# Sparse experts in tiles of 256 rows instead of 128, with the splitting of their weights begun during the routing

## The chip, the cores and the metric

One core of a Trainium2 chip runs the whole program in one launch. The metric is the device time of one execution in microseconds (us). The engines are TensorE (PE, with its weight loads as PEld), VectorE (DVE), ScalarE (ACT), GpSimd (POOL) and SyncE (SP, which issues most DMAs here).

## What is computed

The reference is an audio tower: a tokenizer, then four layers of attention (or a state-space scan) and a feed-forward part, over 32 clips of 93 tokens with 256 features. Each part gets the layer norm of the running sum and is added to it. The change concerns the feed-forward part of the third layer, a mixture of 8 experts of which each token uses the best two:

```python
def _L2_ffn_ref(x, Wr, W1, W2):
    xf = x.reshape(-1, d)
    logits = xf @ Wr
    probs = jax.nn.softmax(logits, axis=-1)
    weights, indices = jax.lax.top_k(probs, TOP_K)
    out = jnp.zeros_like(xf)
    for e in range(n_experts):
        h = jax.nn.gelu(xf @ W1[e], approximate=False) @ W2[e]
        coeff = jnp.sum(jnp.where(indices == e, weights, 0.0), axis=-1)
        out = out + coeff[:, None] * h
    return out.reshape(b, t, d)
```

There are 2976 tokens, so 5952 pairs of a token and an expert. W1 is 256 x 1024 and W2 1024 x 256 for each expert, all in f32.

## The kernel before

The layers run one after the other, each in its own block of five instruction streams, with a barrier between blocks. Streams wait for each other on semaphores that are written out by hand. The mixture (`mixture`) is two blocks, `dispatch` and `expert_tiles`, after the differential attention (`differential_attention`).

**Clearing.** `moe_sent` is a buffer in HBM with a place for every row that any expert may get: `TILES` tiles of 128 rows, where `TILES` is the most that 5952 pairs and eight unfilled last tiles can need, 54. Unused places must hold zeros. The differential attention's SP stream clears the whole buffer (L1406) after its own weight loads and ahead of eight small loads of gamma (L1409). All of that layer's engines wait for `w_loaded`, which counts the gamma loads too.

**Routing (`dispatch`).** In eight groups of four clips VectorE normalises rows (L318), TensorE transposes them (L334), ScalarE copies the result out (L342), TensorE multiplies it by the router's weights (L1668) and VectorE copies the logits (L1691, in `route`). Then VectorE does the softmax, picks the best two, and works out each pair's place among the tiles (L1700 to L1742); TensorE ranks the pairs in between (L1678). Tile t belongs to one expert, whose number is put into `expert[t]`.

**Weights (`dispatch`).** Matmuls here are done in bf16 parts: a f32 matrix is the sum of a high and a low bf16 part, and a product is three matmuls (`split_products`, L1546 to L1548: high by high, high by low, low by high). The weights of the experts are loaded in 32 jobs of 512 KB through four staging buffers (SP, L1618 and L1620). For each, ScalarE makes the high part (L1656) and VectorE the low part by a subtraction (L1750, shown as `moe_w<-route_stage,moe_w`); the buffer is then free for the job four later. ScalarE does its 32 after the softmax's exponential. VectorE does one after each clip's rows in the scatter:

```python
for b in range(B):
    if b >= SENDING:
        dve.wait_ge(rows_sent[b % SENDING], 32 * (b // SENDING))
    dve.tensor_scalar(n.xn[rows, b % SENDING, :], hidden[rows, b, :], ...).then_inc(rows_ready, 1)
    dve.wait_ge(high_ready, b + 1)
    dve.tensor_tensor(weights(b, 1), stage[:, b % STAGES, :], weights(b, 0), ALU.subtract).then_inc(low_ready, 1)
```

**Scatter (`dispatch`).** For each clip VectorE normalises the rows again (L1747) into one of four buffers, and GpSimd sends them by two indirect DMAs (L1641), one for each choice, to their places in `moe_sent`.

**Tiles (`expert_tiles`).** SP loads tile t's rows (L1796). TensorE transposes them (`turn`, L1857), ScalarE and VectorE split them into parts (`take`, L1831 and L1903). `into_hidden` makes 8 blocks of 128 hidden features x 128 rows, each over two halves of 256 features, in three matmuls each: 48 matmuls of 128 columns, with W1 as the stationary operand. ScalarE applies the gelu twice to each half of the hidden sums (L1841 in f32, L1842 as the high part), VectorE subtracts for the low part (L1916). `out_of_hidden` multiplies by W2: 8 x 3 = 24 matmuls of 256 columns, with the activations as the stationary operand. VectorE copies the result (`keep`, L1910), SP stores it (L1800) to `moe_back`. TensorE's order in a tile is `into_hidden(t)`, `turn(t + 1)`, `out_of_hidden(t - 1)`; ahead of each of the two products its sequencer loads the expert's number from `expert` into a register (`value_load`), from which the weights' address is computed. The hidden sums have two sets of two banks in PSUM, so a tile's matmuls need not wait for the last tile's gelu. `over_tiles` makes a loop of it, two tiles a pass.

**Gather.** When all tiles are stored, GpSimd fetches each clip's two sets of rows by 64 indirect DMAs (L1821), and VectorE adds them to the running sum with their weights (L1931).

Of the kernel before, what the change touches and what calls it, by code (L numbers as in the profile page):

```python
# [83 lines left out]
def constants(nc, top, shared):  # L84
# [6 lines left out]
    shared["sent"] = nc.dram_tensor("moe_sent", (TILES * P, D), F32, kind="Internal").ap()  # L91
# [1287 lines left out]
def differential_attention(nc, shared, dram):  # L1379
# [5 lines left out]
    with Scope(nc, "dattn") as s:  # L1385
# [167 lines left out]
TILES = (2 * B * T + EXPERTS * (P - 1)) // P  # L1553


def mixture(nc, shared, dram):

    with Scope(nc, "moe") as s:
# [5 lines left out]
        back = nc.dram_tensor("moe_back", (TILES * P, D), F32, kind="Internal").ap()  # L1564
# [4 lines left out]
def dispatch(nc, shared, dram, w1, w2, slot, share, expert):  # L1569
# [4 lines left out]
    with Scope(nc, "route") as s:  # L1574
# [34 lines left out]
        with nc.Block() as block:  # L1609
# [15 lines left out]
            def _(pool):  # L1625
# [12 lines left out]
                for b in range(B):  # L1638
                    pool.wait_ge(rows_ready, b + 1)
                    for k in range(2):  # L1640
                        pool.indirect_dma_start(sent, bass.IndirectOffsetOnAxis(slot[0:T, k, b:b + 1], 0),  # L1641
                                                n.xn[0:T, b % SENDING, :], None, bounds_check=TILES * P - 1
# [40 lines left out]
            def _(dve):  # L1683
# [3 lines left out]
                def route(g, last):  # L1687
                    if not last:
                        norm_group_dve(dve, n, g + 1, hidden)
# [3 lines left out]

                over_groups(dve, route)
# [14 lines left out]
                dve.sem_inc(chosen_ready, 1)  # L1709

# [8 lines left out]
                steps.link(dve.tensor_scalar(x, upto[:, :, B - 1], 1.0 / P, 1.0 - 1.0 / P - 0.5 + 0.5 / P, ALU.mult, ALU.add))  # L1719
# [4 lines left out]
                steps.link(dve.tensor_scalar(first_slot, x, float(P), None, ALU.mult))  # L1724
# [19 lines left out]
                for b in range(B):  # L1744
# [4 lines left out]
                    dve.wait_ge(high_ready, b + 1)  # L1749
                    dve.tensor_tensor(weights(b, 1), stage[:, b % STAGES, :], weights(b, 0), ALU.subtract).then_inc(low_ready, 1)  # L1750
# [3 lines left out]
def expert_tiles(nc, shared, w1, w2, slot, share, expert, back):  # L1754

    hidden, ident, sent = (shared[k] for k in ("hidden", "ident", "sent"))
    BANK = FC // 2
    RING = 8
    with Scope(nc, "tiles") as s:
        x_in = s.sb("x_in", [P, 2, D])  # L1760
        x_part = s.sb("x_part", [P, 2, 2, DC, P], BF16)
        gelu = s.sb("gelu", [P, 2, BANK, P])
        act1 = s.sb("act1", [P, 2, 2, FC, P], BF16)
        y = s.sb("y", [P, 2, D])
# [25 lines left out]
        with nc.Block() as block:  # L1790
            @block.sync
            def _(sync):
# [12 lines left out]
                def tile(t, j, last):  # L1805
                    if not isinstance(t, int) or t < TILES - 2:
                        load(t + 2, j)
                    if later(t, 1):
                        store(t - 1, 1 - j)
# [848 lines left out]
```

## Time and profile before

| | us |
|---|---|
| median of 3 runs (lowest to highest) | 4664.99 (4653.47 to 4668.2) |
| the profiled execution | 4662.15 |
| its span, first to last instruction | 4660.4 |
| TensorE matmuls busy | 3329.6 (71%) |
| TensorE weight loads busy | 2177.4 (47%) |
| VectorE busy | 2352.3 (50%) |
| GpSimd busy | 1287.5 (28%) |
| ScalarE busy | 1128.7 (24%) |
| routing (2090 to 2155), scatter (2155 to 2285) | 65, 130 |
| expert tiles (2285 to 2749), gather (2749 to 2865) | 464, 116 |

The profile is of one execution. Busy shares are averages over stages that have different limits; a stage's own limit is read from its stretch. Matmuls overlap each other in the array, so the distance between the starts of two of them says more than the duration in their row, whose end is modelled. The idle time in brackets behind a row is that of its engine just before it, with what ended it. "issue" is time in which an engine waited for nothing that the profile shows.

### The profile page before, as it was taken

To read this page: it belongs to the slowest core of one execution; us is meant where nothing else is said; L and a number is where in the kernel's file an instruction comes from. 1 tells how busy PE (TensorE), PEld (TensorE's weight loads), DVE (VectorE), ACT (ScalarE), POOL (GpSimd) and SP (SyncE) were. 2 spreads that over 40 slices of the span, in tenths; PEclk is the share of its full clock that TensorE was granted. 3 is DMA by queue.
4 is the path that set the end of the run, shared out by engine and by line. 5 is a ranking of instruction groups with operands and counts; after the bars stand their busy time and mean duration, and the time that the engine had idled before them with its cause. 6 is when DMAs were issued, how large, how long until landed. Compare 5 with 4: busy or idle time off the path is not lost. (4 is left out here: it accounts for less than half of the span.)

```text
span 4660.4 us, 73226 instructions
## 1 busy us (share of the span) xinstructions
PE 3329.6 (71%) x24055; PEld 2177.4 (47%) x24056; DVE 2352.3 (50%) x4014; ACT 1128.7 (24%) x2258; POOL 1287.5 (28%) x902
## 2 busy tenths in 40 slices
PE   7599935589948999982388852455645565559999
PEld 3367722267735777762266631122222232235677
DVE  0444464234342555544322223788998899861343
ACT  2221200112112222212222210333433343313222
POOL 0111201012110333334400035444554455520121
PEclk9798857778879999995699985677877787769999
DMA  1000003700020000003311111111211121110000
GB/s 41 11 1 0 0 2 70 98 8 0 0 80 0 0 0 0 0 12 100 98 32 32 32 37 50 40 46 34 53 33 40 33 53 33 47 34 0 5 11 11
DMA packets 248269, 136.98 MB, mean 29 GB/s; under 512 B 176065, under 2 KB 224259, under 8 KB 248176
## 3 DMA queue, kind: packets, MB, share of 16 engines
q1 hardware_dynamic: 228272, 119.66, 10.6%
q0 software_dynamic: 18432, 12.40, 1.1%
q10 hardware_dynamic: 1472, 3.85, 0.3%
q8 instruction: 37, 0.61, 0.1%
q14 instruction: 56, 0.46, 0.0%
HBM read 102.36 MB, written 33.31 MB: 29 GB/s over the span
## 5 line engine op out<-in xcount | busy, mean ns | idle before, releaser
L2214 PE MATMUL ssm_y<-ssm_hC,top_ident 128*128 128x512 f32 (+1 forms) x768 | 461.2, 749 | 433.4 <-DVE ssm_hC L2298 432.8
L2083 POOL TENSOR_TENSOR ssm_dBx<-ssm_du,ssm_bc 128x1488 f32<-128x1488 f32 x128 | 543.1, 4255 | 323.2 <-DVE ssm_state L2292 254.8
L2214 PEld LDWEIGHTS ssm_y<-ssm_hC,top_ident 128*128 128x128 f32 x768 | 174.7, 242 | 685.0 <-DVE ssm_hC L2298 457.9
L2292 DVE TENSOR_TENSOR_SCAN ssm_state<-ssm_dA,ssm_dBx 128x744 f32<-128x744 f32 x256 | 421.9, 1689 | 24.7 <-POOL ssm_dBx L2083 11.4
L2155 ACT ACTIVATE ssm_dA<-ssm_delta,ssm_decay 128x368 f32<-128x368 f32 x512 | 270.2, 561 | 657.3 <-DVE ssm_state L2292 565.2
L2298 DVE TENSOR_TENSOR ssm_hC<-ssm_state,ssm_bc 128x1488 f32<-128x1488 f32 x128 | 224.6, 1755 | 4.4
L1821 POOL DMA_INDIRECT tiles_got<-moe_back,moe_slot x64 | 91.5, 1430 | 488.8 <-issue 484.2
L1546 PE MATMUL tiles_hidden<-tiles_x_part,moe_w 128*128 128x128 bf16 x864 | 197.5, 229 | 25.2 <-issue 22.8
L657 ACT ACTIVATE dattn_probs<-dattn_scoresT 93x372 f32<-93x372 f32 x256 | 108.1, 472 | 418.4 <-PE dattn_scoresT L570 418.4
L677 DVE TENSOR_REDUCE dattn_negmax<-dattn_scores 93x4 f32<-93x372 f32 x256 | 127.1, 536 | 161.8 <-PE dattn_scores L542 161.8
L1548 PE MATMUL tiles_hidden<-tiles_x_part,moe_w 128*128 128x128 bf16 x864 | 197.4, 229 | 0.0
L1547 PE MATMUL tiles_hidden<-tiles_x_part,moe_w 128*128 128x128 bf16 x864 | 190.3, 220 | 0.0
L584 PE MATMUL dattn_outputs<-dattn_v,dattn_probs 93*93 (+1 forms) x2048 | 185.8, 233 | 0.0
L584 PEld LDWEIGHTS dattn_outputs<-dattn_v,dattn_probs 93*93 93x93 f32 x2048 | 181.9, 163 | 3.4
L1916 DVE TENSOR_TENSOR tiles_act<-tiles_gelu,tiles_act 128x512 bf16<-128x512 f32 x108 | 74.8, 693 | 212.4 <-ACT tiles_act L1842 212.4
L501 POOL TENSOR_TENSOR rattn_q<-rattn_q_all,rattn_only 128x372 f32<-128x372 f32 x64 | 51.8, 809 | 442.9 <-PE rattn_scoresT L570 246.7
L1420 POOL TENSOR_TENSOR dattn_square<-dattn_square,top_minus_half 93x16 f32<-93x16 f32 x32 | 92.7, 2897 | 290.8 <-DVEq L1496 290.8
L2226 PE MATMUL ssm_misc<-ssm_w_out,ssm_xc 128*93 128x256 f32 x256 | 95.8, 555 | 100.4 <-DVEq L2320 73.8
L501 POOL TENSOR_TENSOR eattn_q<-eattn_q_all,eattn_only 128x372 f32<-128x372 f32 x64 | 51.7, 808 | 404.0 <-PE eattn_scoresT L570 217.0
L501 POOL TENSOR_TENSOR dattn_q<-dattn_q_all,dattn_only 128x744 f32<-128x744 f32 x64 | 91.7, 1433 | 208.6 <-PE dattn_scoresT L570 117.0
L501 POOL TENSOR_TENSOR gattn_q<-gattn_q_all,gattn_only 128x372 f32<-128x372 f32 x64 | 51.8, 809 | 332.4 <-PE gattn_scoresT L570 247.9
L1546 PE MATMUL tiles_product<-moe_w,tiles_act 128*128 x432 | 118.2, 274 | 27.6 <-issue 27.5
(533 smaller groups left out, 7333.6 us busy)
## 6 DMA issues: line engine op xcount, KB each, us to landing
ssm_bc<-dbc_rows SPq DMA_DIRECT2D x128, 372.0 KB, 4.1
route_stage<-in_L_ffn_W SPq DMA_DIRECT2D x32, 512.0 KB, 4.4
qkv_rows<-rattn_rows SPq DMA_DIRECT2D x32, 288.0 KB, 3.0
rattn_heads<-qkv_rows SPq DMA_DIRECT2D x96, 96.0 KB, 3.5
moe_sent<-top_blank SPq DMA_DIRECT2D x1, 6912.0 KB, 20.8
tiles_x_in<-moe_sent SPq DMA_DIRECT2D x54, 128.0 KB, 2.0
moe_back<-tiles_y SPq DMA_DIRECT2D x54, 128.0 KB, 1.7
tok_frames<-in_frames ACTq DMA_DIRECT2D x8, 376.0 KB, 8.5
```

The costliest lines, as they stand in the source:

```text
L501: pool.tensor_tensor(a.q[:, buf, c, :, :], a.q_all[:, c, bass.ds(b * T, T)].unsqueeze(1).broadcast_to([P, a.variants, T]), a.only[:, :].un ...
L584: mm = pe.matmul(a.ps_o[0:T, bank, h * (HD + 1):(h + 1) * (HD + 1)], a.probs[0:T, w % 4, j * T:(j + 1) * T], a.v[0:T, b, h, :], start=True ...
L657: act.activation(a.probs[0:T, w % 4, :], a.ps_t[0:T, w % 2, 0:GT], ACT.Exp, scale=a.exp_scale).then_inc(a.probs_ready, 1)
L677: dve.tensor_reduce(a.negmax[0:T, a.first_map(w):a.first_map(w) + 4], a.ps_s[0:T, w % 2, 0:GT].rearrange("p (j t) -> p j t", j=4), AX.X, A ...
L1546: pe.matmul(out, w_high, x_high, start=start, stop=False)
L1547: pe.matmul(out, w_high, x_low, start=False, stop=False)
L1548: return pe.matmul(out, w_low, x_high, start=False, stop=stop)
L2083: pool.tensor_tensor(dBx[:, k % 2, :, :], du[:, :, :], bc[:, q % 2, 0, k % 2, :].unsqueeze(1).broadcast_to([P, CC, GT]), ALU.mult).then_in ...
L2155: ins = act.activation(dA[:, half, c * GT:(c + 1) * GT].rearrange("p (u t) -> p u t", u=GU)[:, :, 1:], delta[:, 2 * half + c, :].rearrange ...
L2214: mm = pe.matmul(ps_y[:, at], ident[:, :], hC[:, k % 2, :, :].rearrange("p c t -> p (c t)")[:, at], start=(k == 0), stop=(k == N - 1))
L2292: dve.tensor_tensor_scan(state[:, k % 2, chunks, :].rearrange("p c t -> p (c t)"), dA[:, half, 0:HALF], dBx[:, k % 2, chunks, :].rearrange ...
L2298: dve.tensor_tensor(hC[:, k % 2, :, :], state[:, k % 2, :, :], bc[:, q % 2, 1, k % 2, :].unsqueeze(1).broadcast_to([P, CC, GT]), ALU.mult) ...
```

## The change

A tile has 256 rows (`ROWS`), held as two halves of 128 (`HALVES`), and there are 31 tiles, whatever the routing. `moe_sent` and `moe_back` have 7936 rows instead of 6912. In `expert_tiles` a hidden block is 128 features x 256 rows; the hidden sums of one tile fill four banks, of which there is one set; gelu and subtraction work on a bank of two blocks at a time (the same 128x512 shape); the product is made for each half of the rows. TensorE and the other engines still loop over two tiles; SP's stream is written out.

In `dispatch` eight of the 32 splits are moved into the routing loop, one after each group, on ScalarE (`high`) and VectorE (`low`); these loops are written out. VectorE does two more ahead of its wait for the ranks. The other 22 follow the rows of the first 22 clips in the scatter.

```diff
-TILES = (2 * B * T + EXPERTS * (P - 1)) // P
+HALVES = 2
+ROWS = HALVES * P
+TILES = (2 * B * T + EXPERTS * (ROWS - 1)) // ROWS
...
                 sync.dma_start(shared["sent"].rearrange("(a p) d -> p a d", p=P),
-                               shared["blank"][:, :].unsqueeze(1).broadcast_to([P, TILES, D])).then_inc(sent_clear, 16)
+                               shared["blank"][:, :].unsqueeze(1).broadcast_to([P, TILES * HALVES, D])).then_inc(sent_clear, 16)
...
             def _(act):
-                with act.Fori(0, G) as g:
+                def high(k):
+                    act.wait_ge(stage_loaded[k % STAGES], 16 * (k // STAGES + 1))
+                    act.activation(weights(k, 0), stage[:, k % STAGES, :], ACT.Copy).then_inc(high_ready, 1)
+
+                for g in range(G):
                     act.wait_ge(routed, GU * g)
                     norm_group_act(act, n, g, ps_x)
+                    high(g)
                 act.wait_ge(prob_in, 1)
                 act.activation(prob[0:T, :, :], logits[0:T, :, :], ACT.Exp).then_inc(prob_exp, 1)
-                for k in range(JOBS):
-                    act.wait_ge(stage_loaded[k % STAGES], 16 * (k // STAGES + 1))
-                    act.activation(weights(k, 0), stage[:, k % STAGES, :], ACT.Copy).then_inc(high_ready, 1)
+                for k in range(G, JOBS):
+                    high(k)
...
+                def low(k):
+                    dve.wait_ge(high_ready, k + 1)
+                    dve.tensor_tensor(weights(k, 1), stage[:, k % STAGES, :], weights(k, 0), ALU.subtract).then_inc(low_ready, 1)
+
+                for g in range(G):
+                    if g < G - 1:
                         norm_group_dve(dve, n, g + 1, hidden)
                     dve.wait_ge(routed, GU * g + GU)
                     dve.tensor_copy(logits[0:T, bass.ds(GU * g, GU), :],
                                     ps_l[0:T, 0:GU * E].rearrange("p (u e) -> p u e", e=E)).then_inc(logits_ready, 1)
-
-                over_groups(dve, route)
+                    low(g)
...
                 dve.sem_inc(chosen_ready, 1)
+                for k in (G, G + 1):
+                    low(k)
...
-                    dve.wait_ge(high_ready, b + 1)
-                    dve.tensor_tensor(weights(b, 1), stage[:, b % STAGES, :], weights(b, 0), ALU.subtract).then_inc(low_ready, 1)
+                    if G + 2 + b < JOBS:
+                        low(G + 2 + b)
...
-    BANK = FC // 2
+    BANKS, PER = 4, FC // 4
-        ps_h = s.ps("hidden", [P, 2, 2, BANK, P])
-        ps_y = s.ps("product", [P, 2, 512])
+        ps_h = s.ps("hidden", [P, BANKS, PER, ROWS])
+        ps_y = s.ps("product", [P, 2, HALVES, D])
...
                 def into_hidden(t, j):
                     e = pe.value_load(expert[0:1, bass.ds(t, 1)], min_val=0, max_val=EXPERTS - 1)
                     pe.wait_ge(x_low, t + 1)
-                    for half in range(2):
-                        if later(t, 2):
-                            pe.wait_ge(act_high, 2 * t + (half - 3))
-                        for f in range(half * BANK, (half + 1) * BANK):
+                    for q in range(BANKS):
+                        if later(t, 1):
+                            pe.wait_ge(act_high, BANKS * t + (q + 1 - BANKS))
+                        for f in range(PER * q, PER * (q + 1)):
...
-                    for f in range(FC):
-                        if f % BANK == 0:
-                            pe.wait_ge(act_low, 2 * t + (f // BANK + 1))
+                    for h in range(HALVES):
+                        for f in range(FC):
+                            if h == 0 and f % PER == 0:
+                                pe.wait_ge(act_low, BANKS * t + (f // PER + 1))
+                            mm = split_products(pe, ps_y[:, j, h, :], [act1[:, j, part, f, h * P:(h + 1) * P] for part in range(2)],
+                                                [w2[:, part, bass.ds(e, 1), f, :].rearrange("p a n -> p (a n)") for part in range(2)],
+                                                f == 0, f == FC - 1)
```

Three places in the order of the instructions. First SP's queue in the differential attention, where the buffer is cleared:

```order
 L755 DMA dattn_lam<-in_L_attn_lambda_q 93x8
 L755 DMA dattn_lam<-in_L_attn_lambda_k 93x8
-L1406 DMA moe_sent<-top_blank 128x54x256
+L1406 DMA moe_sent<-top_blank 128x62x256
 L1409 DMA dattn_gamma<-in_L_attn_gamma 16x1 x8
 L1399 UNCONDITIONAL_BRANCH
```

Nothing moved; the clearing DMA writes 62 blocks of 128 rows instead of 54, and the gamma loads stand behind it as before.

Second VectorE at the end of the routing's groups, before (the first rows are the end of the loop, `route_logits` are the router's scores, L1700 begins the softmax):

```order
L1691 ISA
L1691 COPY route_logits<-route_scores 93x32
L324 REGISTER_ALU
L324 COMPARE_AND_BRANCH
L1691 COPY route_logits<-route_scores 93x32
L1700 TENSOR_REDUCE route_total<-route_logits 93x32
L1701 TENSOR_TENSOR route_logits<-route_logits,route_total 93x256
L1704 TENSOR_REDUCE route_total<-route_prob 93x32
```

and now:

```order
L318 TENSOR_SCALAR route_xn<-top_hidden,route_mean,route_rstd 93x256 x4
L1701 COPY route_logits<-route_scores 93x32
L1695 TENSOR_TENSOR moe_w<-route_stage,moe_w 128x1024
L1701 COPY route_logits<-route_scores 93x32
L1695 TENSOR_TENSOR moe_w<-route_stage,moe_w 128x1024
L1709 TENSOR_REDUCE route_total<-route_logits 93x32
L1710 TENSOR_TENSOR route_logits<-route_logits,route_total 93x256
L1713 TENSOR_REDUCE route_total<-route_prob 93x32
```

A split (L1695) stands behind each copy of logits, the last one ahead of the softmax's first step.

Third TensorE in a pass of the tile loop, from the last hidden matmuls of a tile to the first product matmuls, before:

```order
L1548 MATMUL tiles_hidden<-tiles_x_part,moe_w 128x128
L1853 ISA
L1857 MATMUL tiles_xturned<-top_ident,tiles_x_in 128x128 x2
L1875 ISA
L1875 TENSOR_LOAD moe_expert
L1875 ISA x2
L1880 ISA
L1546 ISA
L1546 MATMUL tiles_product<-moe_w,tiles_act 128x256
```

and now:

```order
L1548 MATMUL tiles_hidden<-tiles_x_part,moe_w 128x256
L1860 ISA
L1865 MATMUL tiles_xturned<-top_ident,tiles_x_in 128x128 x4
L1883 ISA
L1883 TENSOR_LOAD moe_expert
L1883 ISA x2
L1889 REGISTER_ALU
L1546 ISA
L1546 MATMUL tiles_product<-moe_w,tiles_act 128x256
```

The order is the same; the hidden matmuls have 256 columns, there are four transposes, and the register load (TENSOR_LOAD) stands ahead of the product as before. A pass of the loop has 266 rows of this list before and 320 now.

## Rows read from the trace of the kernel before

**Rows 1.** Stretches (scatter, steady tiles): us, busy us of PE, PEld, DVE, ACT, POOL (x instructions), granted clock, DMA

```profile
2155.00:2285.00 130.00, 0.00 (x0) 0.00 (x0) 51.12 (x63) 29.58 (x28) 105.16 (x64) 0.50 0.57 161
...
2420.00:2520.00 100.00, 88.72 (x880) 68.67 (x879) 26.39 (x47) 28.15 (x58) 0.00 (x0) 1.00 0.10 31
```

**Rows 2.** Timeline, TensorE, first and last tile: start us, us, engine, line, operation [idle before]

```profile
2289.07 0.29 PE L1546 MATMUL tiles_hidden<-tiles_x_part,moe_w 128*128 128x128 bf16 x1 [1.02 <-DVE tiles_x_part L1903]
...
2293.20 0.26 PE L1546 MATMUL tiles_hidden<-tiles_x_part,moe_w 128*128 128x128 bf16 x1
...
2745.89 0.27 PE L1548 MATMUL tiles_product<-moe_w,tiles_act 128*128 x1
```

**Rows 3.** Timeline, TensorE, one tile of the loop

```profile
2320.85 0.23 PE L1546 MATMUL tiles_hidden<-tiles_x_part,moe_w 128*128 128x128 bf16 x1 [0.75 <-issue]
...
2325.17 0.41 PE L1857 MATMUL tiles_xturned<-top_ident,tiles_x_in 128*128 128x128 f32 x2
2326.14 0.28 PE L1546 MATMUL tiles_product<-moe_w,tiles_act 128*128 x1 [0.56 <-issue]
...
2329.22 0.23 PE L1546 MATMUL tiles_hidden<-tiles_x_part,moe_w 128*128 128x128 bf16 x1 [0.25 <-issue]
```

**Rows 4.** Timeline, TensorE, within a hidden and a product phase

```profile
2500.92 0.23 PE L1546 MATMUL tiles_hidden<-tiles_x_part,moe_w 128*128 128x128 bf16 x1
...
2501.92 0.23 PE L1546 MATMUL tiles_hidden<-tiles_x_part,moe_w 128*128 128x128 bf16 x1
...
2504.31 0.27 PE L1546 MATMUL tiles_product<-moe_w,tiles_act 128*128 x1
...
2506.49 0.27 PE L1548 MATMUL tiles_product<-moe_w,tiles_act 128*128 x1
```

**Rows 5.** Timeline, TensorE, end of the stage: hidden to product, product to product

```profile
2739.52 0.23 PE L1548 MATMUL tiles_hidden<-tiles_x_part,moe_w 128*128 128x128 bf16 x1
2740.43 0.28 PE L1546 MATMUL tiles_product<-moe_w,tiles_act 128*128 x1 [0.68 <-issue]
...
2742.96 0.27 PE L1548 MATMUL tiles_product<-moe_w,tiles_act 128*128 x1
2743.35 0.28 PE L1546 MATMUL tiles_product<-moe_w,tiles_act 128*128 x1
```

**Rows 6.** Scatter: GpSimd in the timeline; groups by line (busy us, mean ns | idle before)

```profile
2155.48 5.82 POOL L1641 DMA_INDIRECT moe_sent<-route_xn,moe_slot  x1 [57.09 <-issue]
...
2174.53 2.12 POOL L1641 DMA_INDIRECT moe_sent<-route_xn,moe_slot  x1 [0.30 <-DVE route_xn L1747]
...
L1641 POOL DMA_INDIRECT moe_sent<-route_xn,moe_slot x64 | 105.2, 1643 | 76.3 <-issue 72.0 <-DVE route_xn L1747 4.3
L1750 DVE TENSOR_TENSOR moe_w<-route_stage,moe_w 128x1024 bf16<-128x1024 f32 x32 | 38.7, 1211 | 0.0
```

**Rows 7.** Groups by line in the tile stage, ScalarE

```profile
L1842 ACT ACTIVATE tiles_act<-tiles_hidden 128x512 bf16<-128x512 f32 x108 | 64.5, 597 | 0.0
...
L1831 ACT ACTIVATE tiles_x_part<-tiles_xturned 128x256 bf16<-128x256 f32 x54 | 20.7, 384 | 98.0 <-PE tiles_xturned L1857 98.0
```

**Rows 8.** DMA issues of the page (KB each, us to landing); timeline, VectorE, attention layer

```profile
moe_sent<-top_blank SPq DMA_DIRECT2D x1, 6912.0 KB, 20.8
...
1391.09 0.16 DVE L1460 TENSOR_TENSOR dattn_lam<-dattn_lam 93x8 f32<-93x8 f32 x1 [24.46 <-DMA dattn_gamma<-in_L_attn_gamma]
```

**Rows 9.** DMA issues of the page: loads of a tile

```profile
tiles_x_in<-moe_sent SPq DMA_DIRECT2D x54, 128.0 KB, 2.0
```

**Rows 10.** Timeline, routing: ScalarE, VectorE in a group; VectorE after the ranks

```profile
2125.49 0.85 ACT L342 ACTIVATE route_xT<-route_xturned 128x372 f32<-128x372 f32 x2 [4.10 <-PE route_xturned L334]
2125.64 1.38 DVE L318 TENSOR_SCALAR route_xn<-top_hidden,route_mean,route_rstd 93x256 f32 x4 [1.18 <-PE route_xturned L334]
...
2144.18 0.42 DVE L1715 COPY route_choice_left<-route_rank 93x256 f32<-93x256 f32 x1 [2.23 <-PE route_rank L1678]
```

**Rows 11.** DMA queues, tile stage: packets, MB, share of 16 engines

```profile
q8 instruction: 5, 0.08, 0.1%
```

More of the change, by code:

```diff
@@ L1795, in load @@
                         sync.wait_ge(x_turned, t - 1)
-                    sync.dma_start(x_in[:, j, :], sent[bass.ds(t * P, P), :]).then_inc(x_loaded[j], 16)
+                    sync.dma_start(x_in[:, j, :, :], rows_of(sent, t)).then_inc(x_loaded[j], 16)
                 def store(t, j):
                     sync.wait_ge(y_copied, t + 2)
-                    sync.dma_start(back[bass.ds(t * P, P), :], y[:, j, :]).then_inc(y_stored[j], 16)
+                    sync.dma_start(rows_of(back, t), y[:, j, :, :]).then_inc(y_stored[j], 16)
                 load(0, 0)
                 load(1, 1)
[L1805 to L1809, printed above, removed]
-                over_tiles(sync, tile)
-                store(TILES - 1, 1)
+                for t in range(TILES):
+                    if t < TILES - 2:
+                        load(t + 2, t % 2)
+                    if t:
+                        store(t - 1, (t - 1) % 2)
+                store(TILES - 1, (TILES - 1) % 2)
             @block.gpsimd
@@ L1829, in take @@
                     if later(t, 2):
[L1830 to L1832 removed]
+                        act.wait_ge(h_done, BANKS * (t - 1))
+                    act.activation(x_part[:, j, 0, :, :], ps_x[:, j, :, :], ACT.Copy).then_inc(x_high, 1)
                 def tile(t, j, last):
[L1835 to L1838 removed]
+                    for q in range(BANKS):
+                        act.wait_ge(h_done, BANKS * t + (q + 1))
+                        if later(t, 1) or q >= 2:
+                            act.wait_ge(act_low, BANKS * t + (q - 1))
                         if later(t, 2):
                             act.wait_ge(y_done, t - 1)
[L1841 to L1844 removed]
+                        act.activation(gelu[:, q % 2, :, :], ps_h[:, q, :, :], ACT.Gelu)
+                        act.activation(act1[:, j, 0, PER * q:PER * (q + 1), :], ps_h[:, q, :, :], ACT.Gelu).then_inc(act_high, 1)
+                        if q == BANKS - 2 and not last:
                             take(t + 1, 1 - j)
@@ L1877, in out_of_hidden @@
                         pe.wait_ge(y_copied, t)
[L1878 to L1883 removed]
+                    for h in range(HALVES):
+                        for f in range(FC):
[4 more added lines that the diff above has]
+                                                f == 0, f == FC - 1)
                     mm.then_inc(y_done, 1)
@@ L1909, in keep @@
                         dve.wait_ge(y_stored[j], 8 * (t - j))
-                    dve.tensor_copy(y[:, j, :], ps_y[:, j, 0:D]).then_inc(y_copied, 1)
+                    dve.tensor_copy(y[:, j, :, :], ps_y[:, j, :, :]).then_inc(y_copied, 1)
                 def tile(t, j, last):
-                    for half in range(2):
-                        dve.wait_ge(act_high, 2 * t + (half + 1))
-                        at = slice(half * BANK, (half + 1) * BANK)
-                        dve.tensor_tensor(act1[:, j, 1, at, :], gelu[:, half, :, :], act1[:, j, 0, at, :],
+                    for q in range(BANKS):
+                        dve.wait_ge(act_high, BANKS * t + (q + 1))
+                        at = slice(PER * q, PER * (q + 1))
+                        dve.tensor_tensor(act1[:, j, 1, at, :], gelu[:, q % 2, :, :], act1[:, j, 0, at, :],
                                           ALU.subtract).then_inc(act_low, 1)
-                        if half == 0 and not last:
+                        if q == BANKS - 2 and not last:
                             take(t + 1, 1 - j)
```

60 lines of the change are left out of this document (22 added, 38 removed).

## The prediction

> **What bounds the kernel now.** I read the profile's first line, then the table of stretches, then the rows of each stretch that the change touches. The span is 4660.4 us and the execution's own time 4662.15 us, 2.8 us under the median of the runs shown (4664.99 us); the sum below is made against 4662.15. Between runs 0.3% (14 us) is about what this kernel's measurement can tell from no change.
>
> Three stretches are touched. In the tile stage the reader is to see TensorE busy 88.72 us of 100 at a granted clock of 1.00, the others under a third [rows 1]: TensorE sets the pace. It runs from the first hidden matmul at 2289.07 to the start of the last product matmul at 2745.89 [rows 2], so 54 tiles take 456.9 us with the last matmul's pitch, 8.46 us each. In the scatter before it, TensorE has nothing to do and GpSimd is busy 105.16 us of 130 [rows 1] with 64 indirect DMAs [rows 6]: GpSimd sets the pace there. And the attention layer before (differential_attention) starts only when VectorE has the gamma loads, for which it waits 24.46 us [rows 8].
>
> **Inside a tile.** A tile has 48 hidden matmuls of 128 columns, 2 transposes, 24 product matmuls of 256 columns. Hidden start to transposes is 4.32 us, transposes to product 0.97, product to the next hidden 3.08 [rows 3]. From 2500.92 to 2501.92 twelve hidden matmuls start: 0.083 us each. From 2504.31 to 2506.49 twenty product matmuls: 0.109 us each [rows 4]. Why are 128 columns not half of 256? At the end of the stage hidden matmuls are followed directly by a product: last start 2739.52, next 2740.43, 0.91 us, which is 0.83 more than a pitch. Two products follow each other with 0.39 us (2742.96 to 2743.35), 0.28 more than a pitch [rows 5]. Both times the same register load of the expert's number stands between. I read this so: TensorE's instruction stream needs 0.083 us per matmul. Hidden matmuls of 128 columns wait for it, so no lead builds up and the load is paid in full (0.83). Product matmuls of 256 columns take 0.109 in the array, the stream gains 24 x 0.026 = 0.62 us on it, and pays only the rest (0.83 - 0.62 = 0.21, measured 0.28).
>
> **The change, tile stage.** 54 tiles of 74 TensorE operations (3996) become 31 of 100 (3100). Every matmul now has 256 columns.
> - Hidden: 48 x 0.109 = 5.23 us.
> - Transposes: 4 instead of 2. The two take 0.41 us as one row [rows 3] with the modelled tail in it; I take 0.7 for four (bounds 0.5 and 0.85).
> - Product: 2 halves x 24 x 0.109 = 5.23 us.
> - Gaps: before, 0.97 - 0.41 = 0.56 ahead of the product and 3.08 - 24 x 0.109 = 0.46 ahead of the hidden matmuls [rows 3]. Now the stream gains 48 x 0.026 = 1.25 us in each phase, more than the 0.83 that a load costs, so both gaps should be covered: 0.2 us are left for both. Upper bound: both stay, 1.0.
>
> Sum 5.23 + 0.7 + 5.23 + 0.2 = 11.4 us a tile (bounds 11.0 and 12.3); x 31 = 353 us. The nearest row for the gap is the product followed by a product, where a lead of 0.62 took away two thirds; a lead of 1.25 is twice that.
>
> What must stay hidden: the hidden sums now have one set of four banks, so TensorE must not overtake ScalarE. ScalarE's two passes over 512 columns take 0.597 us each [rows 7], four banks 4.8 us, and the copy of x (0.384 for 256 columns, about 0.6 for 512) makes 5.4 of 11.4. The last bank is read only after the next tile's transposes, by about 8 us into the tile, and TensorE wants that bank 11.4 + 3.9 us into it: 7 us of slack. The loads of x (2.0 us for 128 KB [rows 9], at most twice that for 256 KB) stand in SP's queue behind the store of an older tile and still have more than a tile's time. If this cover were gone, each us would be paid 31 times.
>
> Edges, once: the stage starts cold. From 2289.07 to 2293.20, 39 matmuls start [rows 2], 0.106 each, after a stretch at clock 0.50, the 1.2 GHz level [rows 1]. With 256 columns that time passes at an estimated 0.213, some 2 us lost; the second tile's wait for its x (1.02 us before, in the same row's place) grows to about 1.6; the first load and copies are 1.3 longer, the last copy and store 0.7. Together 6 us. Stage: 353 + 6 = 359 against 457: **-98 us.**
>
> Here a rule speaks for another pace. The measured row is 0.109 us for 256 columns [rows 4]. The Trainium skill, TensorE: Matmul & The Clock Gate, section Back-to-back issue gap, gives about 81 ns at 128 columns and 131 at 512 in a real stream of loads and matmuls. The trace agrees at 128 (0.083), but a straight line between the two would be 98 ns at 256, an estimate of that page, and the trace has 109. By the page the tile would be 1.1 us shorter and the whole 33 us; the measured row decides.
>
> **The change, scatter.** Each of 64 issues costs 1.31 + 0.30 us where nothing disturbs it, 103 us; busy and idle of the group without the first wait make 105.2 + 76.3 - 57.1 = 124.4 [rows 6]. The first issue accounts for 4.5 of the excess (5.82, while VectorE runs its first burst of four rows and four weight parts), which stays. The other 16.5 us lie in issues of 2.1 to 2.6 us like the one at 2174.53, which starts right after VectorE's row copy, as VectorE goes on with a weight part (0.81 longer). Of 28 weight parts in the steady loop 18 remain: 16.5 x 10/28 = 5.9, taken as **-5 us**. Bounds: nothing, if the loads of the weights and not VectorE lengthen the issues, and -13 (ten times 1.3).
>
> **The change, routing.** Eight splits go into the routing loop. ScalarE idles 4.10 us a group there and VectorE 1.18 after its logits copy [rows 10]; VectorE's half of a split takes 1.21 us [rows 6], and ScalarE's, one pass over the same 128x1024, is far under 4. So they are hidden but for some 0.05 us of VectorE's, which delay rows that TensorE wants later still; their cover is TensorE's chain of scores and transposes. Only the eighth stands between the last copy and the softmax: +1.2 us. Two more fill VectorE's wait of 2.23 us for the ranks [rows 10] and need 2.4: +0.2. The table of tiles is shorter (31 columns for 54): -0.4. **+1 us.** The weight loads that SP sends earlier land while the queue is otherwise empty.
>
> **The change, clearing.** moe_sent grows from 6912 to 7936 KB. The eight gamma loads stand behind it in SP's queue; it lands after 20.8 us and VectorE starts right behind [rows 8]. 20.8 x 8/54 = **+3 us**, all on the path (bounds 0 and 3.5). The gather after the stage has the same 64 indirect DMAs: nothing.
>
> Sum: -98 - 5 + 1 + 3 = -99. 4662 - 99 = 4563 us; with the 2 to 3 us to the median, **4564 us.**
>
> **The rivals.**
> 1. *The gaps stay* (a register load costs its time whatever the lead). A tile is 12.3 us, 31 x 0.9 = 28 us more: 4592. For it: a product followed by a product still shows 0.28 us [rows 5]. Against: that 0.28 is a third of the 0.83 without lead. If the pauses of the hidden phase stay as well (4.32 - 48 x 0.083 = 0.34 for two halves, 0.7 for four banks), 22 us more: 4614.
> 2. *A hidden matmul of 256 columns is faster than a product one*, because its pace is set by the stream and not by the array. Between the 0.083 and the 0.109 [rows 4] lies 0.096; in the hidden phase alone that is 31 x 48 x 0.013 = 19 us less, 4545, and in both phases 39 us, 4525. Against it stands the steady 0.109 of twenty matmuls with the same number of columns. The page's figure above points this way.
> 3. *The loop no longer stays in the instruction buffer.* TensorE's loop over two tiles grows from 266 to 320 rows of the list of instructions. Before, 25 passes brought only 5 instruction fetches of 16 KB in the whole stage [rows 11], so the loop was not fetched again. If it were now, each of 14 passes would pay up to three fetches in series, 2.0 us each by the nearest row, a small load [rows 9]: 84 us, 4648. The Trainium skill, Runtime: NRT & Kernel Launch, Instruction fetch mechanics, says that a taken branch to code outside the buffer forces a fetch, and gives TensorE a larger buffer (128 KiB) than the other engines in one line and two 16 KiB lines in another; the few fetches here agree with a loop that fits.
> 4. *The splits begun early give nothing*: the scatter is bound by its own issue or its DMAs. 4569; inside the forecast's range.
> 5. *Slower: the clock.* If TensorE were granted 1.2 GHz in the tile stage, a matmul would take an estimated 0.213 and a tile 11.4 + 96 x 0.104 = 21.4 us: 310 us more, 4874. It decides from 99/310, about a third, of the stage at the low level. Its place would be a wait for x or for ScalarE in every tile, long enough to idle TensorE. For it: the stage starts at that level after an idle stretch. Against: the clock stayed at 1.00 with two gaps of half a us in every tile [rows 1], and now there are fewer gaps.
>
> **How the numbers follow.** Forecast 0.66 (own range 4545 to 4576, from the bounds of transposes and scatter); gaps stay 0.15, pauses too 0.05; faster matmuls 0.05; refetching 0.04; nothing from the early splits 0.03; clock 0.02. The range 4544 to 4600 holds the forecast, the gaps that stay and rival 4: 0.84. Over 0.3% faster is all but the clock and part of the refetching: 0.95; within 0.3% 0.02; slower 0.03.
>
> **What would show it.** Right: hidden matmuls at 0.109, a tile period of 11.2 to 11.7 us at clock 1.00, no issue gaps of half a us ahead of product or hidden; undisturbed issues of 1.31 us in the last ten pairs of the scatter; gamma about 3 us later. Wrong: periods of 12.3 us or more, VectorE or ScalarE named as releaser of hidden matmuls, or instruction fetches in every pass.

## The result and the profile after

| us | before | changed |
|---|---|---|
| median (lowest to highest) | 4665.84 (4653.47 to 4668.2, 4 runs) | 4544.84 (4541.94 to 4550.9, 4 runs) |
| span of the profiled execution | 4660.4 | 4541.6 |
| ratio of the times, 95% interval | | 0.9748, 0.9727 to 0.9768 |

The change saves 121 us; 99 to 101 were forecast. The time lies 19 us under the forecast, inside the range of 4544 to 4600 by 0.8 us; two of the four runs (4541.94 and 4543.29) lie below it.

The table of stretches of the changed kernel, scatter and steady tiles, to be read against [rows 1] (us, busy us of PE, PEld, DVE, ACT, POOL with their instructions, granted clock, DMA share, GB/s):

```profile
2148.00:2275.00 127.00, 0.00 (x0) 0.00 (x0) 39.89 (x55) 19.01 (x18) 101.16 (x64) 0.50 0.44 123
...
2400.00:2500.00 100.00, 100.00 (x919) 90.04 (x917) 37.55 (x55) 44.37 (x83) 0.00 (x0) 1.00 0.16 49
```

TensorE was busy 88.72 us of 100 and is now busy all of them, at a clock of 1.00. Its timeline shows the start of the stage, then one steady tile, then the stage's last row (start, us, engine, line, operation, idle before); [rows 2, 3] answer to them:

```profile
2280.77 0.39 PE L1546 MATMUL tiles_hidden<-tiles_x_part,moe_w 128*128 128x256 bf16 x1 [1.50 <-DVE tiles_x_part L1912]
...
2284.58 0.36 PE L1546 MATMUL tiles_hidden<-tiles_x_part,moe_w 128*128 128x256 bf16 x1
2284.77 0.27 PE L1547 MATMUL tiles_hidden<-tiles_x_part,moe_w 128*128 128x256 bf16 x1
...
2290.03 0.28 PE L1546 MATMUL tiles_hidden<-tiles_x_part,moe_w 128*128 128x256 bf16 x1 [1.50 <-DVE tiles_x_part L1912]
...
2453.79 0.27 PE L1546 MATMUL tiles_hidden<-tiles_x_part,moe_w 128*128 128x256 bf16 x1
...
2459.03 0.60 PE L1865 MATMUL tiles_xturned<-top_ident,tiles_x_in 128*128 128x128 f32 x4
2459.47 0.27 PE L1546 MATMUL tiles_product<-moe_w,tiles_act 128*128 x1
...
2464.71 0.27 PE L1546 MATMUL tiles_hidden<-tiles_x_part,moe_w 128*128 128x256 bf16 x1
...
2622.24 0.27 PE L1548 MATMUL tiles_product<-moe_w,tiles_act 128*128 x1
```

The steady tile takes 2464.71 - 2453.79 = 10.92 us: 5.24 + 0.44 + 5.24. That is 100 operations of 0.109 us with nothing between them; the pauses of half a us in [rows 3] are gone. The last product starts at 2622.24, so 31 tiles take 341.6 us where 54 took 456.9: -115.3. The cold start is the 0.21 us pitch of the first 18 matmuls, at a granted clock of 0.50 (the 1.2 GHz level).

The scatter's group by line (busy us, mean ns | idle before), to [rows 6]:

```profile
L1643 POOL DMA_INDIRECT moe_sent<-route_xn,moe_slot x64 | 101.2, 1581 | 77.4 <-issue 74.1 <-DVE route_xn L1758 3.4
```

The clearing among the DMA issues (KB, us to landing), to [rows 8]:

```profile
moe_sent<-top_blank SPq DMA_DIRECT2D x1, 7936.0 KB, 23.6
```

VectorE's timeline at the start of the attention layer, in a routing group and at the ranks, to [rows 8, 10]:

```profile
1385.37 0.16 DVE L1460 TENSOR_TENSOR dattn_lam<-dattn_lam 93x8 f32<-93x8 f32 x1 [27.17 <-DMA dattn_gamma<-in_L_attn_gamma]
...
2102.45 0.19 DVE L1701 COPY route_logits<-route_scores 93x32 f32<-93x32 f32 x1 [2.22 <-PE route_scores L1674]
2102.56 1.21 DVE L1695 TENSOR_TENSOR moe_w<-route_stage,moe_w 128x1024 bf16<-128x1024 f32 x1
...
2136.58 2.36 DVE L1695 TENSOR_TENSOR moe_w<-route_stage,moe_w 128x1024 bf16<-128x1024 f32 x2 [0.15 <-DVE route_chosen L1530]
2138.86 0.42 DVE L1726 COPY route_choice_left<-route_rank 93x256 f32<-93x256 f32 x1
```

GpSimd's issues take 101.2 us where they took 105.2. VectorE waits 27.17 us for gamma, 2.71 more. In the routing it still waits 2.22 us for TensorE after a split, so that split was hidden; the copy of the ranks is no longer waited for.

Stage by stage in the two profiles (first to last row of each): routing 64.2 to 65.3, scatter 124.4 to 120.4, from there to the first hidden matmul 9.2 to 10.8, tiles -115.3, gather 118.2 to 116.5. With the 2.7 of the clearing that is -115.6 us of the 118.8 by which the two spans differ. The other 3 us lie in layers that the change doesn't touch, within the scatter of the profiles: over the 14 profiles of this study the attention layer begins at 1354.5 to 1370.3 us, and the state-space layer takes 1270 to 1280.

### The profile page after: what moved, and what is told of

The parts are those of the page before. It is cut to its first block and busy times, and to the rows that moved or that the text cites. A ratio compares the mean times of both kernels' runs of the same rounds, so it can differ in the third digit from the quotient of the medians.

```text
span 4541.6 us, 69496 instructions
## 1 busy us (share of the span) xinstructions
PE 3260.2 (72%) x23159; PEld 2164.5 (48%) x23160; DVE 2360.9 (52%) x3984; ACT 1144.9 (25%) x2267; POOL 1283.4 (28%) x902
## 5 line engine op out<-in xcount | busy, mean ns | idle before, releaser
L2300 DVE TENSOR_TENSOR_SCAN ssm_state<-ssm_dA,ssm_dBx 128x744 f32<-128x744 f32 x256 | 421.8, 1688 | 24.4 <-POOL ssm_dBx L2091 11.4
L501 POOL TENSOR_TENSOR dattn_q<-dattn_q_all,dattn_only 128x744 f32<-128x744 f32 x64 | 91.6, 1431 | 210.2 <-PE dattn_scoresT L570 115.6
L1924 DVE TENSOR_TENSOR tiles_act<-tiles_gelu,tiles_act 128x512 bf16<-128x512 f32 x124 | 85.8, 692 | 101.8 <-ACT tiles_act L1850 101.8
L1546 PE MATMUL tiles_hidden<-tiles_x_part,moe_w 128*128 128x256 bf16 x496 | 136.2, 274 | 3.0 <-DVE tiles_x_part L1912 3.0
L1547 PE MATMUL tiles_hidden<-tiles_x_part,moe_w 128*128 128x256 bf16 x496 | 136.1, 274 | 0.0
L1548 PE MATMUL tiles_hidden<-tiles_x_part,moe_w 128*128 128x256 bf16 x496 | 136.1, 274 | 0.0
L1547 PE MATMUL tiles_product<-moe_w,tiles_act 128*128 x496 | 135.2, 273 | 0.0
```

What stands on the lines that cost most here:

```text
L501: pool.tensor_tensor(a.q[:, buf, c, :, :], a.q_all[:, c, bass.ds(b * T, T)].unsqueeze(1).broadcast_to([P, a.variants, T]), a.only[:, :].un ...
L1546: pe.matmul(out, w_high, x_high, start=start, stop=False)
L1547: pe.matmul(out, w_high, x_low, start=False, stop=False)
L1548: return pe.matmul(out, w_low, x_high, start=False, stop=stop)
L2300: dve.tensor_tensor_scan(state[:, k % 2, chunks, :].rearrange("p c t -> p (c t)"), dA[:, half, 0:HALF], dBx[:, k % 2, chunks, :].rearrange ...
```

## Experiments on the tile stage

The table is worked out from the traces. Tile stage is from the first hidden to the last product matmul; the phases are medians from start to start.

| run | median us | ratio to before (95%) | tile stage | hidden | transposes | product |
|---|---|---|---|---|---|---|
| before | | | 456.8 | 4.29 | 0.89 | 3.11 |
| keep_before | 4619.31 | 0.9904 (0.9882 to 0.9925) | 410.7 | 4.30 | 0.33 | 2.85 |
| fixed_before | 4517.31 | 0.969 (0.9666 to 0.9714) | 300.4 | 2.68 | 0.22 | 2.62 |
| changed | 4544.84 | 0.9748 (0.9727 to 0.9768) | 341.5 | 5.24 | 0.44 | 5.24 |
| keep_after | 4540.41 | 0.9744 (0.9714 to 0.9773) | 340.9 | 5.24 | 0.44 | 5.24 |
| loads2 | 4549.97 | 0.9764 (0.9735 to 0.9793) | 348.7 | 5.24 | 0.51 | 5.28 |
| loads3 | 4586.6 | 0.9843 (0.9814 to 0.9871) | 386.2 | 5.25 | 1.32 | 5.74 |
| narrow | 4542.79 | 0.9745 (0.9714 to 0.9776) | 345.3 | 5.36 | 0.44 | 5.24 |
| narrow_twin | 4643.56 | 0.9963 (0.9939 to 0.9987) | 434.3 | 7.92 | 0.88 | 5.26 |

**Is it the instruction stream?** On the kernel before, both phases took the first expert's weights, so the choice of the expert is left out, and with it every register load and address step of the tiles:

```diff
-e = pe.value_load(expert[0:1, bass.ds(t, 1)], min_val=0, max_val=EXPERTS - 1)
+e = 0
```

> The kernel before with the first expert's weights for every tile: neither register loads nor address arithmetic in TensorE's stream; which expert computes a row is left out. My theory (the 0.083 us of a hidden matmul is the pace of the instruction stream, two address steps for three matmuls): hidden matmuls at about 0.055 us, no gaps of half a us, a tile of 5.4 to 6 us instead of 8.46, 130 to 165 us less, about 4515 us. Rival (0.083 is what the array needs for a weight load and 128 columns): only the loads go, some 45 us less, hidden matmuls stay at 0.083.

The timeline of one of its tiles, with the last hidden matmul as second row:

```profile
2452.11 0.22 PE L1546 MATMUL tiles_hidden<-tiles_x_part,moe_w 128*128 128x128 bf16 x1
...
2454.73 0.22 PE L1548 MATMUL tiles_hidden<-tiles_x_part,moe_w 128*128 128x128 bf16 x1
2454.79 0.39 PE L1857 MATMUL tiles_xturned<-top_ident,tiles_x_in 128*128 128x128 f32 x2
2455.02 0.27 PE L1546 MATMUL tiles_product<-moe_w,tiles_act 128*128 128x256 bf16 x1
```

The same 48 hidden matmuls take 2.62 us for 47 pitches, 0.056 each. So 0.083 was not the array's pace with 128 columns; the rival falls. The tile stage is 156 us shorter than before: 87 of these lie in the hidden phases, 36 between the transposes and the product, 33 from the product to the next hidden matmul. It is even 41 us shorter than the changed kernel's: 54 x 128 = 6912 rows are less work than 31 x 256 = 7936. The change thus trades 156 us of loads and address steps for 41 us of work on 1024 more rows that stay unfilled; that is its 115.

**Is a load paid before, and covered now?** The register that the hidden phase loaded is kept for the product, in both kernels:

```diff
-e = pe.value_load(expert[0:1, bass.ds(t, 1)], min_val=0, max_val=EXPERTS - 1)
+e = pe.snap(kept[j], min_val=0, max_val=EXPERTS - 1)
```

> The kernel before with one register load less in a tile: the expert's number that was loaded ahead of the hidden matmuls is kept in one of two registers for the product of the same tile, and the range checks of the loads are gone. My theory (hidden matmuls of 128 columns wait for the instruction stream, so a load behind them is paid in full): the time from the transposes to the product falls from 0.97 to about 0.35 us, 0.6 us in 54 tiles, 33 us less, and up to 45 with the checks. Rival (the gap is a wait for the split activations or for the turned x): no change.

> The changed kernel with one register load less in a tile, the same edit as on the kernel before. My theory (the loads are covered): no change, tile period 10.92 us. Rival (a part of a load is still paid): 31 x 0.1 us or more less.

One edit, two answers: 46 us of tile stage in the kernel before (0.57 us at the transposes and 0.27 in the product phase, 54 times), 0.6 us in the changed one. Both as expected. The edit also takes out the range checks, so the 46 us are the price of one load and of the checks of two.

**How much does the lead cover?** The loads were done twice and three times (a loop around the same line).

> The changed kernel with every register load of the expert's number done twice. My theory (the stream gains 0.026 us on the array in each matmul of 256 columns and so covers what stands in it): an extra load is 0.65 to 0.83 us of stream, a tile's stream 10.9 to 11.6 us against 10.92 in the array: nothing to 22 us more. Rival (a load shows in full whatever the lead): 2 x 0.65 to 0.83 in 31 tiles, 40 to 51 us more.

> The changed kernel with every register load done three times. My theory: a tile's stream is now 12.2 to 13.3 us and sets the pace instead of the array: 40 to 73 us more, and the gaps ahead of hidden and product matmuls are back, while matmuls between them stay at 0.109 us or are still at the array's pace after a gap. Rival 1 (a load shows in full): 81 to 103 us more. Rival 2 (loads are always hidden beside matmuls of 256 columns): no change.

A tile of loads3, from its timeline:

```profile
2464.54 0.60 PE L1865 MATMUL tiles_xturned<-top_ident,tiles_x_in 128*128 128x128 f32 x4
2465.93 0.28 PE L1546 MATMUL tiles_product<-moe_w,tiles_act 128*128 x1 [0.78 <-DVE tiles_act L1926]
...
2471.09 0.27 PE L1548 MATMUL tiles_product<-moe_w,tiles_act 128*128 x1
2471.60 0.28 PE L1546 MATMUL tiles_hidden<-tiles_x_part,moe_w 128*128 128x256 bf16 x1 [0.24 <-issue]
```

The pauses are back. The profile names a VectorE step for the first of them, but only the loads differ from the changed kernel, so they are its cause. The step from two to three loads costs (386.2 - 348.7) / 31 / 2 = 0.60 us each; the step from one to two costs 0.12 each. So a phase covers one load and nearly a second, no more. Both rivals (always paid, always hidden) fall.

Why no more, the loads themselves show. The trace has them as instructions of TensorE's sequencer (PEldq), which runs the stream ahead of the array. The loads ahead of one product in the kernel before, in the changed kernel and in loads3 (count, duration in ns, first and last start):

```profile
L1875 PEldq TENSOR_LOAD <-moe_expert x1: 297/297/297, 2325.3 to 2325.3; - x1
```

```profile
L1883 PEldq TENSOR_LOAD <-moe_expert x1: 302/302/302, 2457.8 to 2457.8; - x1
```

```profile
L1885 PEldq TENSOR_LOAD <-moe_expert x3: 296/297/299, 2463.8 to 2465.1; - x3
```

In the kernel before the load starts behind the last hidden matmul and 0.84 us ahead of the first product matmul at 2326.14 [rows 3]: there is no lead, and the load is paid. In the changed kernel it starts 1.7 us ahead of the product at 2459.47, with 15 matmuls and transposes still to start. Over all its tiles from the third on the lead at a load is 13 to 17 of them. In narrow (below), with hidden matmuls half as wide, it is 15 to 17 ahead of the product as well, though that is only 0.98 to 1.20 us. So the lead ends at some 17 matmuls, at either width. Loads done again follow each other at about 0.65 us. In loads3 the first product matmul starts 2.15 us after the first load, and a lead of 11 or 12 matmuls of 0.109 covers 1.2 to 1.3 us of it. What is left is the pause (1.32 us from the transposes to the product, where the changed kernel has 0.44).

**Width or count?** Each hidden matmul of the changed kernel was cut into two of 128 columns:

```diff
-for c in range(DC):
-    mm = split_products(..., x_part[:, j, part, c, :], ...)
+for h, c in ((h, c) for h in range(HALVES) for c in range(DC)):
+    mm = split_products(..., x_part[:, j, part, c, h * P:(h + 1) * P], ...)
```

> The changed kernel, tiles of 256 rows, with each hidden matmul cut into two of 128 columns: 96 instead of 48 in a tile, everything else the same. My theory (the width of the matmuls is what matters): 96 x 0.083 = 8.0 us for the hidden phase, the load ahead of the product shows again with about 0.6 us, a tile of about 14.1 us, 31 x 3.2 = 99 us more than the changed kernel, some 4645 us. Rival (the gain comes from having fewer tiles, with fewer loads, waits and transposes): at most 20 us more.

A miss: 96 matmuls of 128 columns take 5.36 us, 0.056 each, and the time doesn't change. My theory of a price per matmul falls. The rival's number came true, but fewer loads, waits and transposes can't be the whole reason, since in fixed_before the hidden phase itself fell from 4.29 to 2.68 us. The order of TensorE's instructions in narrow tells what I had missed; each ISA row works out an address from the expert's number:

```
L1546 ISA
L1546 MATMUL tiles_hidden<-tiles_x_part,moe_w 128x128
L1547 MATMUL tiles_hidden<-tiles_x_part,moe_w 128x128
L1548 ISA
L1548 MATMUL tiles_hidden<-tiles_x_part,moe_w 128x128
L1546 MATMUL tiles_hidden<-tiles_x_part,moe_w 128x128
L1547 MATMUL tiles_hidden<-tiles_x_part,moe_w 128x128
L1548 MATMUL tiles_hidden<-tiles_x_part,moe_w 128x128
```

The second half of the rows uses the addresses of the first: 32 steps for 96 matmuls, where the kernel before has 32 for 48. The new theory is a price per address step: 3 matmuls of 0.083 have two steps, 0.124 each. narrow_twin keeps everything of narrow and only makes the second half work its addresses out again:

```diff
+pe.reg_mov(copy, e)
+twin = (e, pe.snap(copy, min_val=0, max_val=EXPERTS - 1))
...
-w1[:, part, bass.ds(e, 1), c, f * P:(f + 1) * P]
+w1[:, part, bass.ds(twin[h], 1), c, f * P:(f + 1) * P]
```

> As narrow, 96 hidden matmuls of 128 columns in a tile of 256 rows, but the second half of the rows takes the weights' addresses from a copy of the register, so that they are worked out again: 64 address steps in a hidden phase instead of 32; matmuls, waits and data are the same. My theory after narrow (not a matmul costs stream time but an address step, 0.124 us each): the hidden phase grows from 5.36 to 64 x 0.124 = 7.9 us and a little more, the load ahead of the product finds no lead and shows with 0.6 to 0.7 us, a tile takes about 14.4 us instead of 11.04, 31 x 3.4 = 105 us more than narrow, some 4645 us, tile stage about 448 us. Rival (128 columns are cheap whenever a tile has 256 rows, through the banks or the shape of the phase): no change against narrow, 4543 us.

One tile of narrow, then one of narrow_twin:

```profile
2463.12 0.22 PE L1546 MATMUL tiles_hidden<-tiles_x_part,moe_w 128*128 128x128 bf16 x1
...
2468.48 0.61 PE L1865 MATMUL tiles_xturned<-top_ident,tiles_x_in 128*128 128x128 f32 x4
2468.92 0.27 PE L1546 MATMUL tiles_product<-moe_w,tiles_act 128*128 x1
```

```profile
2499.68 0.22 PE L1546 MATMUL tiles_hidden<-tiles_x_part,moe_w 128*128 128x128 bf16 x1
...
2507.22 0.63 PE L1865 MATMUL tiles_xturned<-top_ident,tiles_x_in 128*128 128x128 f32 x4
2508.09 0.28 PE L1546 MATMUL tiles_product<-moe_w,tiles_act 128*128 x1 [0.24 <-issue]
...
2513.35 0.22 PE L1546 MATMUL tiles_hidden<-tiles_x_part,moe_w 128*128 128x128 bf16 x1
```

The hidden phase is 7.54 us here and 7.93 in the next tile, in turn, against 64 x 0.124 = 7.94. The pause ahead of the product is back (0.87 from the transposes, 0.44 in narrow). Same matmuls, same tiles, same waits, and 89 us more in the tile stage, 434 us where 448 were expected; that the whole, 4643.56 us, comes so close to the expected 4645 is luck. So address steps set the pace of the hidden phase, and tiles of 256 rows use each step for twice the rows. With keep_before it follows that the kernel before was bound by its address steps (the 87 us of the hidden phases) and by the register loads between the phases (most of the other 69).

## Experiments on the scatter and the clearing

tiles_only takes the early splits out of the changed kernel (all 32 follow the rows again); splits_only puts them into the kernel before; after_again is the changed kernel, measured beside the others.

> The changed kernel without the early splits: all 32 splits follow the rows of the scatter again, as before. If the tiles carry the gain (my theory), the tile stage stays at a period of 10.92 us and about 341 us, the scatter is back at 124 us (120 with the early splits), the routing back at 64 us (65), so 3 us more than the changed kernel, some 4548 us. If the early splits carried a part that the stages hide (rival), the time is more than 10 us above the changed kernel's.

> The kernel before with the early splits alone, tiles of 128 rows. My theory: routing 1 us longer, scatter 4 us shorter, tile stage 457 us as before: 3 us less, 4662 us, not to be told from no change by its time. Rival: the early splits carry a share of the change's 121 us: more than 10 us less.

> The changed kernel once more, as the yardstick for the three others: 4545 us within 10, tile period 10.92 us, scatter 120.4 us, routing 65.3 us.

| run | median us (lowest to highest) | ratio to before (95%) | routing | scatter |
|---|---|---|---|---|
| tiles_only | 4559.01 (4548.48 to 4562.62) | 0.9767 (0.9748 to 0.9786) | 64.1 | 128.7 |
| splits_only | 4661.53 (4651.49 to 4671.46) | 0.9996 (0.9984 to 1.0008) | 65.8 | 119.0 |
| after_again | 4546.12 (4544.4 to 4549.45) | 0.9741 (0.9724 to 0.9757) | 65.3 | 120.4 |
| gamma_first | 4536.22 (4526.77 to 4543.22) | 0.9721 (0.9701 to 0.9741) | 65.3 | 120.2 |
| two_splits | 4534.96 (4531.22 to 4543.29) | 0.9717 (0.97 to 0.9735) | 66.4 | 115.2 |

after_again repeats the changed kernel's time and stages. The tiles carry the gain: alone they leave 97.7% of the time, and the splits alone can't be told from no change. By its median tiles_only is 13 us slower than after_again, more than the rival's 10, and the stages explain 7 of it (1.2 less in the routing, 8.3 more in the scatter). The intervals of the two overlap, and the two profiled executions lie the other way round (4548.48 and 4549.45), so it stays open whether the early splits carry more than that beside tiles of 256 rows. In the kernel before they don't (splits_only). Over all profiles the scatter takes 124.4 to 128.7 us with 32 splits beside it (four runs) and 118.2 to 122.3 with 22 (nine runs): the early splits are worth some 6 us there, and cost 1 in the routing. That the splits beside them lengthen GpSimd's issues is plain in the last 20 issues of the changed kernel, which have none left: 1.31 to 1.43 us each and 32.2 in all, where the kernel before took 36.4 and tiles_only 38.6.

gamma_first puts the eight gamma loads ahead of the clearing in SP's queue (two statements change places), and two_splits does two splits in each routing group besides (`high(2 * g)`, `high(2 * g + 1)`, and `low` likewise).

> The changed kernel with the eight gamma loads ahead of the clearing in SP's queue. If the clearing lies on the path (my theory), VectorE's wait for gamma of 27.17 us shrinks by the most of the clearing's 23.6 us, down to what the weight loads and GpSimd's constants (until about 16 us into the layer) leave: 10 to 18 us less in the attention layer, some 4530 us. Rival: the layer's weight loads end just as late, and nothing is gained.

> As the kernel with gamma first, and two splits in each routing group instead of one, so that 18 instead of 10 are done before the scatter. If VectorE's weight parts lengthen GpSimd's issues (my theory), 14 instead of 22 of them are left beside the scatter, which then takes about 117 us instead of 120.4; VectorE's wait of 2.2 us in each routing group covers the second split's 1.21 us, so the routing is at most 2 us longer. Rival: the weights' loads cannot follow (1 MB in a group of 5 us), and the routing grows by more than the scatter shrinks.

VectorE and GpSimd at the start of the attention layer in gamma_first:

```profile
1363.85 0.16 DVE L1460 TENSOR_TENSOR dattn_lam<-dattn_lam 93x8 f32<-93x8 f32 x1 [7.73 <-DMA dattn_gamma<-in_L_attn_gamma]
...
1365.12 7.37 DVE L318 TENSOR_SCALAR dattn_xn<-top_hidden,dattn_mean,dattn_rstd 93x256 f32<-93x256 f32 x4
...
1365.75 6.10 POOL L452 TENSOR_SCALAR_AFFINE_SELECT dattn_sel<-dattn_sel 128x2976 bf16<-128x2976 bf16 x2
```

The wait for gamma falls by 19.4 us, so the clearing was on the path. But the four row copies behind it, 1.38 us in the changed kernel, now meet GpSimd's mask and take 7.37. The layer takes 718.6 us here and 714.2 in two_splits, against 723.0 to 731.1 in the twelve profiles with the old order, 725 in the middle: a gain of 6 and 11 us, where 10 to 18 were expected. What VectorE no longer waits for gamma it loses in part to the mask. In two_splits the scatter takes 115.2 us (about 117 were expected) and the routing is 1 longer, as expected. Its slowest run is 1.1 us faster than the fastest of after_again, and its median 11 us: the best kernel of the study with the full computation, though the 95% intervals of the two ratios overlap. Its gain over gamma_first is not shown by the times.

## Why the prediction was right, and where it was off

- **What bounds** held: TensorE sets the pace of the tile stage (before, its instruction stream; now, the array); GpSimd that of the scatter, VectorE's wait for gamma the start of the attention layer. The sign named for the scatter came true (the last 20 issues above). That for the tile, a period of 11.2 to 11.7 us, did not.
- **Hidden and product phases**, 5.23 us each: measured 5.24.
- **Mis-sized: "Transposes ... I take 0.7 for four (bounds 0.5 and 0.85)" and "0.2 us are left for both" gaps.** Four transposes take 0.44, 0.109 each as every other operation: the 0.41 of the row for two held the modelled tail, and I had not taken it off. Both gaps are nothing. The tile is 10.92 us and not 11.4, below my lower bound of 11.0; 31 x 0.48 = 15 us of the 19. So the time lies inside the range by luck: it is below the forecast's own range of 4545 to 4576, and the bounds from which that was taken (0.5 and 0.85 for the transposes, nothing and -13 for the scatter) give only 4550 to 4574.
- **Mis-sized: the edges**, "together 6 us". 341.6 - 31 x 10.92 = 3 us inside the stage, with the cold pitch and the second tile's wait for x (1.50 in the row at 2290.03, 1.6 expected); the 1.6 us more ahead of it are given back by a gather 1.7 shorter.
- **Failed in its reason: "TensorE's instruction stream needs 0.083 us per matmul".** The runs show 0.124 for an address step, of which three matmuls need two. The sum didn't suffer, and that was luck: the changed kernel happens to have 32 steps in a hidden phase, and 32 x 0.124 make the same 4.0 us as 48 x 0.083, beside matmuls of twice the columns. What I worked out from it for narrow did. "The stream gains 48 x 0.026 = 1.25 us" was right in kind, as both gaps are covered, but not in its reason: the lead is 13 to 17 matmuls (1.44 to 1.95 us) in both phases, and ends there although the 16 steps of a product phase (2.0 us of 5.24) would let it grow further.
- **128 and 256 columns.** The kernel before had 0.083 us at 128 columns; without address steps (fixed_before), or with 32 for 96 matmuls (narrow), they take 0.056, and at 256 columns at 0.109. The Trainium skill, TensorE: Matmul & The Clock Gate, section Back-to-back issue gap, gives about 81 ns at 128 columns for a stream of loads and matmuls. The row's 0.083 agreed with it by accident, and the 0.056 does not agree. For 256 columns the row's 0.109 decided rightly against the 98 ns estimated from that section of the Trainium skill. Another formula of the same section of the Trainium skill, N / 2.4 + 2.5 ns, there kept for isolated matmuls, gives 56 and 109 ns. These are what the streams here show.
- **Scatter** -5: measured -4.0, and -6 over all profiles. The 16.5 us of lengthened issues in its working should read 16.9 (124.4 - 103 - 4.5), which changes nothing. **Routing** +1: measured 1.1. **Clearing** +3: measured 2.7.
- **Rivals.** The gaps did not stay (1), no phase of matmuls of 256 columns went below 0.109 (2), the tile stage still has five instruction fetches (3; the queue's row reads as in [rows 11]), the early splits gave 4 us and not nothing (4), and the clock of the steady tiles stayed at 1.00 (5).

Open: why the lead ends at some 17 matmuls; no run tested it. Nor was a kernel tried that has tiles of 128 rows and fewer address steps. By fixed_before, which has none, it could win at most another 41 us of the tile stage.

## What to carry to other kernels

Where a busy engine shows pauses marked as issue and a pitch that the same operation undercuts elsewhere, count the address and register steps between its instructions: their price (0.124 us a step, 0.6 a load) lies beside the matmuls only as long as these are wide enough, and a lead of at most some 17 matmuls must cover it. A tile that is twice as wide uses each step twice, but it also pads more rows, so sparing the steps themselves could be better still (fixed_before's tile stage is 41 us shorter). And a large clearing in a queue should stand behind the small loads that a layer starts with.

## What was not expected of the hardware

A transpose of 128 columns in f32 takes as long as a bf16 matmul of 256 columns, 0.109 us in the stream. TensorE is busy 100 us of 100 with hidden matmuls of 128 columns (fixed_before, narrow) as with 256, once the address steps and loads take less time than the array. The stream's lead ends at some 17 matmuls with 128 columns (narrow) as with 256 (the changed kernel). And VectorE's row copies took 6.0 us longer beside GpSimd's two mask instructions, which take 6.10 (7.37 for copies of 1.38): it stood still for them. The Trainium skill, SBUF — State Buffer, section Terms, says that of the port pair which VectorE and GpSimd share the loser fully blocks; the trace agrees here.
